# Two graph layers on one core: node tiles computed between the edge groups of the first layer

## Chip, cores and metric

One NeuronCore of a Trainium2 chip runs the whole program. The metric is the device time in microseconds (us) of one launch. Everything is float32.

## What is computed

There are 3125 nodes with 160 features (64 scalars, and 32 vectors of 3 components stored as `D = 64 + 96` columns) and 100,000 edges sorted by `dst`. Two message-passing layers follow each other, each with a residual and a layer norm. Cut to what matters here:

```python
# layer 0: gather f at src, sum over edges into dst
f_s, f_v = x_s @ Wl1_0 * a/8, einsum(x_v, Wl1_1) * a/sqrt(32)    # "f0", a = node_vec1
w0, w1, w2, w3 = split(gelu(gelu(ea8 @ Wfc1) @ Wfc2) @ Wfc3)
gs, gv = f_s[src], f_v[src];  y0, y1 = ea4[:, 0], ea4[:, 1:4]
mid0 = w0 * gs * y0
mid1 = w3 * einsum('euc,ec->eu', gv, y1) / sqrt(3)               # the dot product
mid2 = (w1 * gs)[:, :, None] * y1[:, None, :]
mid3 = w2[:, :, None] * gv * y0[:, None, None]
ns0, ns1, nv2, nv3 = segment_sum(..., dst) / sqrt(32)
x1 = layernorm(x + self_connection + alpha * out)                # per node; small matmuls of the sums
# layer 1: project x1, gather at dst, sum over edges into src
s, v, skip = x1 @ W_nl, x1 @ W_skip                              # per node
tp = tensor_product(relu(ea64 @ W_fc1) @ W_fc2, s[dst], v[dst], direction(ea3))
agg = segment_sum(tp, src);  out = layernorm(x1 + gate(agg @ W_out + skip))
```

## The kernel before

Edges are taken in groups of 512 (`G = 4` tiles of 128), 196 groups (`NGRP`). Nodes stand in 25 tiles of 128 rows (`NT`), in 5 chunks of 5 (`NC`, `FT`). Each engine has its own program; semaphores order them. The program has four stages.

**Prologue** (a block of its own, ended by a barrier of all engines). SP loads indices, then the small weights, then x; ACT's queue loads x transposed in two transfers. PE projects each node tile with both weight pairs side by side, so `ps_n` holds `f0` and the self connection; ACT scales the first half to `frow` (L293) and stores a chunk to `f0` in memory (L297); DVE adds the second half to `xres` (L382). Two PSUM buffers, so PE waits for both readers. POOL clears constants and the accumulators `acc_a`, `acc_b`, `acc_c`. DVE converts indices, counts whether every group's targets fit a window of 24 nodes (`win_ok`; with these inputs they do, so the `fast()` paths run), and works out edge directions in rows for a later table (`row_squares` to `row_dirs`).

**First layer**, 196 steps. POOL sends 4 indirect gathers for each group (L693), four groups ahead at most: group u waits for `prod_done` of group u - 4. PE runs three small MLP layers (`ps_h1`, `ps_h2` in a bank each, `ps_w`), ACT the two gelus. DVE builds a one-hot `ohot` and `sel` (one-hot times the 4 values of ea4), then three products of weights and gathered rows: `ta` (two copies of the scalars), `tb` (w3 times the 3 vector components) and `tc` (w2 times them). PE sums them into node windows (`window_sums`, L909): `ta` against all 4 copies of `sel`, `tb` against one, `tc` against three, 12 matmuls of two passes each. DVE adds the windows to the three accumulators (L1172). The dot product is thus taken after the sum over edges: ACT copies the diagonal blocks of `acc_c` onto each other later (L818). SP meanwhile clears the four output tables and writes the tables `hot_dst` and `hot_dir`.

**Node stage**, between joins 1 and 2 of all engines: for each node tile PE multiplies the sums (`update`), DVE adds to `xres`, takes mean and variance, ACT the square root, DVE a Newton step and the norm; PE transposes (`turn`) and projects (`project`); ACT copies out (`out_rows`), POOL spreads the row into `fst` (L716 to L724), SP stores it to `feat` and the skip part to table 0. Edge directions are worked out here too.

**Second layer**, 392 pairs of edge tiles (`NPAIR`): PE picks rows of `feat` with a one-hot (`window_gather`), forms the message; POOL adds messages into four tables in memory (L740, two indirect transfers a pair). An output stage adds the tables, gates and normalises.

The gather of the first layer, whose pace matters below:

```python
def gather(u, j, r):
    if r % 4 == 0:
        since(pool, gidx_done, j * 4 + r // 4 + 1)
    since(pool, prod_done, u - 3)
    for k in range(G):
        pool.indirect_dma_start(out=gat[:, r % 4, k, :], in_=t["f0"], ...).then_inc(gath[r % 4], 16)
```

## Time and profile before

| what | us |
|---|---|
| median of 3 runs (2736.01 to 2775.7) | 2751.35 |
| the profiled execution | 2767.32 |
| its span on the core | 2765.5 |

Times in the profile are microseconds from the start of the span. PE is TensorE's matmul, PEld its weight load, DVE VectorE, ACT ScalarE, POOL GpSimd, SP the engine that mostly issues transfers; SPq, ACTq are their transfer queues. PEclk is the granted TensorE clock as a share of full speed; 0.50 and 1.00 are its two levels. A row with xN merges N instructions from the start shown; "idle before <-" names what ended the idle time of the engine.

### The profile page before, as it was taken

The numbers are of one execution on the slowest core, as the hardware profiler recorded it, in microseconds if no ns is written. First come the engines' busy times: TensorE is split into PE (matmuls) and PEld (weight loads), VectorE is DVE, ScalarE is ACT, GpSimd is POOL, SyncE is SP. The second block draws the span as 40 slices with busy tenths as digits, with TensorE's granted clock in tenths as the row PEclk, the third lists the DMA queues.
The fourth block names the chain that finished last, engine by engine and source line by source line (L and its number), as shares of the span: only waits on it lengthen the run. The fifth ranks groups of instructions, "written<-read, shape, count | busy, mean of one in ns | idle before, by whom it ended". The sixth has DMA issues, their size and how long they took to land.

```text
span 2765.5 us, 80992 instructions
## 1 busy us (share of the span) xinstructions
PE 2655.6 (96%) x24330; PEld 2250.7 (81%) x24330; DVE 1649.6 (60%) x4264; ACT 899.5 (33%) x2015; POOL 2063.6 (75%) x1856
## 2 busy tenths in 40 slices
PE   4799999999999999999999999999999999999996
PEld 2477777777777777979999999999999999999993
DVE  5365555556555555526666666666666666666664
ACT  1111111111111112224444444444444444444442
POOL 3477777777777775247888888888888888888884
PEclk9999799889989898659999999999999999999998
DMA  4343343333433333247888888888888888888877
GB/s 132 111 110 105 100 109 106 100 104 105 108 103 105 105 105 85 104 173 142 141 144 144 141 144 143 144 143 143 143 142 143 143 144 142 144 144 142 144 124 189
DMA packets 388993, 355.59 MB, mean 129 GB/s; under 512 B 60992, under 2 KB 340928, under 8 KB 388416
## 3 DMA queue, kind: packets, MB, share of 16 engines
q0 software_dynamic: 150528, 141.40, 34.9%
q1 hardware_dynamic: 234816, 209.69, 27.2%
q10 hardware_dynamic: 3616, 4.11, 0.6%
q8 instruction: 15, 0.25, 0.0%
q14 instruction: 18, 0.15, 0.0%
HBM read 244.75 MB, written 135.90 MB: 138 GB/s over the span
## 4 chain that ended last, share of the span: by engine, by line
PE 65%; POOL 16%; issue 11%; DMA 3%; DVE 1%; DVEq 0%; ACT 0%; SPq 0%; POOLq 0%; ACTq 0%
POOL gat L693 15%; PE ps_o L1062 13%; PE ps_w L1050 12%; PE ps_d L1071 10%; PE ps_o L1060 9%; PE ps_x L1084 6%; PE ps_g L909 4%; PE ps_x L1024 3%; DMA gat<-f,gidx 2%; PE ps_w L935 2%; PE ps_h L928 1%; PE ps_h L923 1%; PE ps_r L981 1%; DMA tab<-summed,sidx 1%; PE ps_y L998 1%
## 5 line engine op out<-in xcount | busy, mean ns | idle before, releaser
L740 POOL DMA_INDIRECT tab<-summed,sidx x784 | 1218.6, 1554 | 264.5 <-issue 212.7
L693 POOL DMA_INDIRECT gat<-f,gidx x784 | 751.8, 959 | 244.8 <-issue 232.0
L1291 DVE TENSOR_TENSOR prod<-ps_w,xg 128x768 f32<-128x768 f32 x392 | 375.4, 958 | 244.5 <-PE ps_w L1050 226.7
L1062 PE MATMUL ps_o<-ro_v,prod 128*128 128x96 f32 x3136 | 478.5, 275 | 0.0
L1062 PEld LDWEIGHTS ps_o<-ro_v,prod 128*128 128x128 f32 x3136 | 413.3, 192 | 0.0
L1050 PE MATMUL ps_w<-hid,wf 64*128 64x128 f32 x4704 | 369.3, 290 | 2.0 <-ACT hid L864 2.0
L863 ACT ACTIVATE xg<-ps_x 128x768 f32<-128x768 f32 x392 | 296.3, 808 | 198.8 <-PE ps_x L1084 189.4
L1050 PEld LDWEIGHTS ps_w<-hid,wf 64*128 64x128 f32 x4704 | 294.1, 188 | 70.2 <-issue 44.6
L1071 PE MATMUL ps_d<-msg,same 128*128 128x193 f32 x1568 | 332.5, 334 | 0.7 <-ACT summed L882 0.7
L1060 PE MATMUL ps_o<-ro_s,prod 96*128 96x96 f32 x1568 | 330.2, 292 | 0.6 <-DVE msg L1302 0.6
L909 PEld LDWEIGHTS ps_g<-sel,ta 128*128 128x128 f32 x1568 | 210.0, 209 | 95.0 <-issue 59.2
L1160 DVE TENSOR_TENSOR ta<-ps_w,gat 128x512 f32<-128x512 f32 x196 | 135.5, 691 | 253.6 <-DMA gat<-f,gidx 191.2
L1060 PEld LDWEIGHTS ps_o<-ro_s,prod 96*128 96x128 f32 x1568 | 235.8, 190 | 48.1 <-issue 0.9
L876 ACT ACTIVATE msg<-ps_o 128x192 f32<-128x192 f32 x392 | 130.2, 332 | 443.6 <-PE ps_o L1062 424.5
L909 PE MATMUL ps_g<-sel,ta 128*128 128x96 f32 x1568 | 244.1, 304 | 21.3 <-DVE acc_c L1172 21.1
L785 ACT ACTIVATE h<-ps_h 128x256 f32<-128x256 f32 x196 | 75.1, 383 | 581.8 <-PE ps_h L928 576.8
L1071 PEld LDWEIGHTS ps_d<-msg,same 128*128 128x128 f32 x1568 | 247.9, 192 | 0.9 <-DVE msg L1302 0.9
L882 ACT ACTIVATE summed<-ps_d 128x386 f32<-128x386 f32 x392 | 193.1, 492 | 159.7 <-DMA tab<-summed,sidx 81.7
L1298 DVE TENSOR_TENSOR ash<-ps_o,sh 128x192 f32<-128x192 f32 x392 | 140.1, 357 | 137.6 <-ACT msg L876 131.1
L935 PE MATMUL ps_w<-w,h 64*128 64x192 f32 x1568 | 207.5, 388 | 0.0
L935 PEld LDWEIGHTS ps_w<-w,h 64*128 64x128 f32 x1568 | 143.2, 211 | 76.4 <-issue 76.4
L909 PE MATMUL ps_g<-sel,tc 128*96 128x72 f32 x1568 | 192.9, 272 | 0.0
(198 smaller groups left out, 3416.9 us busy)
## 6 DMA issues: line engine op xcount, KB each, us to landing
src_bc<-in_src_rows SPq DMA_DIRECT2D x196, 256.0 KB
tabw<-feat SPq DMA_DIRECT2D x784, 36.0 KB
ea<-in_ea SPq DMA_DIRECT2D x196, 128.0 KB
feat<-fst SPq DMA_DIRECT2D x25, 576.0 KB, 2.9
gat<-f,gidx POOLq DMA_INDIRECT x784
hot_dst<-in_dst_rows SPq DMA_DIRECT2D x98, 128.0 KB
hot_dir<-sh_rows SPq DMA_DIRECT2D x98, 128.0 KB
dst_bc<-hot_dst SPq DMA_DIRECT2D x196, 64.0 KB
```

What stands on the lines that cost most here:

```text
L693: pool.indirect_dma_start(out=gat[:, r % 4, k, :], out_offset=None, in_=t["f0"], in_offset=bass.IndirectOffsetOnAxis(ap=gidx[:, r // 4, at ...
L740: pool.indirect_dma_start(out=t["tabs"][into[k]], out_offset=bass.IndirectOffsetOnAxis(ap=sidx[:, r, k:k + 1], axis=0), in_=summed[:, r, k ...
L863: act.activation(xg[:, r, 2 * i:2 * i + 2, :], ps_x4[:, 2 * i:2 * i + 2, 0:3 * P], ACT.Copy)
L882: act.activation(summed[:, ur, :, :], ps_d[:, :, 0:LW], ACT.Copy).then_inc(sum_done, 1)
L909: last = pe.matmul(ps_g[r][0:hi, (n * 4 + lo) * WIN:(n * 4 + up) * WIN], lhs[:, r, k, :, :].rearrange("p a b -> p (a b)"), sel[:, r, k, lo ...
L935: last = pe.matmul(ps_w[r][:, k, 0:192], h2[h:h + S, r, P * (k % 2):P * (k % 2) + P], w3[h:h + S, :], start=True, stop=True)
L1050: last = pe.matmul(ps_w4[:, h, P * c:P * c + P], wf2[rows_h, c, :], hid[rows_h, r // 2, at], start=True, stop=True)
L1060: pe.matmul(ps_o[:, k, 0:96], prod[0:96, ur % 2, k, 0, :], ro_s[0:96, :], start=True, stop=True)
L1062: last = pe.matmul(ps_o[:, k, 96 + 64 * c:192 + 64 * c], prod[:, ur % 2, k, 1 + c, :], ro_v[:, c, :], start=True, stop=True)
L1071: last = pe.matmul(ps_d[:, k, 0:LW], same[:, ur // 2, ur % 2 * 2 + k, :], msg[:, ur % 2, k, :], start=True, stop=True)
L1084: last = pe.matmul(ps_x4[:, k, P * c:P * c + P], tabw[rows_k, r, CHUNK[c]:CHUNK[c] + P], hot[rows_k, r, :], start=True, stop=True)
L1291: dve.tensor_tensor(prod[:, r % 2, :, :, :].rearrange("p k c e -> p k (c e)"), ps_w4[:, :, 0:3 * P], xg[:, r // 2, r % 2 * 2:r % 2 * 2 + 2 ...
```

## The change

1. Prologue: weights are loaded first, x transposed comes in five pieces on ACT's queue. PE projects `f0` for all 25 tiles (`ps_n`, 4 buffers) before it projects the self connection for all 25 (`ps_m`, 3 buffers). ACT does its square roots after `f0`. POOL clears more (staging, weights, one accumulator of 5 x 3200) and then sends the first sixteen gathers (groups 0 to 3) inside the prologue, once `f0` is stored; `gather` skips them later. `win_ok` gains a check that the targets rise evenly enough.
2. First layer: DVE takes the dot product for each edge. `vy` = vectors times y1, `dot` its sum over components; `wy` = w2 times y0; `tb` now holds 3 blocks `wy * gv` and a fourth, w3 times `dot`. `window_sums` is 4 matmuls of `ta` against `sel` and 4 of `tb` against `ohot`; one accumulator `acc` and one addition a group. `ps_h1` and `ps_h2` share a bank, and `layer1(u)` waits for the second gelu of the group before.
3. Node tiles are worked on in the edge loop, now unrolled by 8 (`PER`): tile t gets its sums copied out at DVE's step 8(t+1)+5 (`node_parts`), PE's `update`, `turn`, `project` at steps 0, 4, 6 of block t+2, DVE's `node_update`, `node_scale`, `node_norm`, `node_turned`, `node_staged` at 0, 1, 2, 4, 6, and ACT's spreading into `fst` and store to `feat` at steps 2 to 4 of block t+3 (POOL has no part in it). The inverse root is made on DVE alone, from a shift and three Newton steps. 23 tiles go through the loop, the last two into the first pairs of the second layer. Loads of later weights go into the loop's first steps. One join is left of two.
4. The skip part goes to table 0 in ten transfers on SP's queue in the second layer's first steps; the scatters start with tables 2 and 3, and pair 1 waits for all ten.

The diff, cut to its core:

```diff
 @block.gpsimd  (prologue)
+                pool.memset(fst[:, :, :, :], 0.0).then_inc(fst_zero, 1)
+                pool.memset(acc[:, :, :], 0.0).then_inc(zeroed, 1)
...
+                pool.wait_ge(gidx_done, 1)
+                pool.wait_ge(f_out[0], 16 * (-(-NC // 2)))
+                pool.wait_ge(f_out[1], 16 * (NC // 2))
+                for u in range(4):
+                    for k in range(G):
+                        pool.indirect_dma_start(
+                            out=gat[:, u, k, :], out_offset=None, in_=t["f0"],
...
 @block.tensor  (prologue)
                 for u in range(NT):
...
+                    since(pe, f_ready, u - 3)
+                    pe.matmul(ps_n[u % 4][:, 0:S], xt_s[:, here], w_s2[:, 0, :], start=True, stop=True)
+                    pe.matmul(ps_n[u % 4][:, S:D], xt_v[:, here], w_v2[:, 0, :], start=True, stop=True).then_inc(n_ready, 1)
+                for u in range(NT):
+                    since(pe, res_ready, u - 2)
+                    pe.matmul(ps_m[u % 3][:, 0:S], xt_s[:, here], w_s2[:, 1, :], start=True, stop=True)
+                    pe.matmul(ps_m[u % 3][:, S:D], xt_v[:, here], w_v2[:, 1, :], start=True, stop=True).then_inc(m_ready, 1)
 def window_sums(pe, r, ready):
-                for n, (lhs, hi, lo, up) in enumerate(((ta, P, 0, 4), (tb, 96, 0, 1), (tc, 96, 1, 4))):
-                    for k in range(G):
-                        last = pe.matmul(ps_g[r][0:hi, (n * 4 + lo) * WIN:(n * 4 + up) * WIN],
...
+                for k in range(G):
+                    pe.matmul(ps_g[r][:, 0:4 * WIN], ta[:, r, k, :, :].rearrange("p a b -> p (a b)"),
+                              sel[:, r, k, :, :].rearrange("p a b -> p (a b)"), start=k == 0, stop=k == G - 1)
+                for k in range(G):
+                    last = pe.matmul(ps_g[r][:, 4 * WIN:5 * WIN], tb[:, r, k, :, :].rearrange("p a b -> p (a b)"),
+                                     ohot[:, r, k, :], start=k == 0, stop=k == G - 1)
 def layer1(u, r, j):
-                    since(pe, g1_done, u)
+                    since(pe, g2_done, u)
 def products(u, j, r):   (DVE)
+                    dve.tensor_tensor(vy[:, :, :, :], gv, y[:, bass.ds(u * G, G), 1:4]..., ALU.mult).then_inc(vy_done, 1)
                     dve.wait_ge(w_ready, u + 1)
                     dve.tensor_tensor(ta[:, h, :, :, :], ...)
+                    dve.tensor_tensor(wy[:, :, :], ps_w[h][:, :, 2 * S:2 * S + V], ...).then_inc(wy_done, 1)
+                    dve.wait_ge(vy_done, u + 1)
+                    dve.tensor_reduce(dot[:, :, :], vy[...].rearrange("p k c u -> p k u c"), AX.X, ALU.add).then_inc(dot_done, 1)
+                    dve.wait_ge(wy_done, u + 1)
+                    dve.tensor_tensor(tb[:, h, :, 0:3, :], wy[:, :, :].unsqueeze(2)..., gv, ALU.mult)
+                    dve.wait_ge(dot_done, u + 1)
+                    dve.tensor_tensor(tb[:, h, :, 3, :], ps_w[h][:, :, 2 * S + V:2 * S + 2 * V], dot[:, :, :],
+                                      ALU.mult).then_inc(prod_done, 1)
 def fast(), step(s, j, r):   (DVE)
+                        if r == 5 and (not isinstance(j, int) or 0 <= j - 1 < TIN):
+                            since(dve, acc_done, s - 1)
+                            node_parts(j - 1)
+                        tile = j - 2
+                        if not isinstance(tile, int) or 0 <= tile < TIN:
+                            if r == 0:
+                                node_update(tile, 0)
+                            if r == 1:
+                                node_scale(tile, 1)
+                            if r == 2:
+                                node_norm(tile, 1)
+                            if r == 4:
+                                node_turned(tile, 0)
+                            if r == 6:
+                                node_staged(tile, 0)
+                def node_parts(u):
+                    dve.tensor_copy(tile_sums[:, :, :], acc[:, :, here]).then_inc(part_done, 1)
+                def node_scale(u, n):
+                    linked(last)
+                    linked(dve.tensor_scalar(var, mv[:, 0:n, 1], EPS, None, ALU.add))
+                    linked(dve.tensor_scalar(tmp.bitcast(I32), var.bitcast(I32), 1, None, ALU.logical_shift_right))
+                    linked(dve.tensor_scalar(y.bitcast(I32), tmp.bitcast(I32), -1.0, float(0x5f3759df), ALU.mult, ALU.add))
+                    for _ in range(2):
+                        linked(dve.tensor_tensor(tmp, y, y, ALU.mult))
+                        linked(dve.tensor_tensor(tmp, tmp, var, ALU.mult))
+                        linked(dve.tensor_scalar(tmp, tmp, -0.5, 1.5, ALU.mult, ALU.add))
+                        linked(dve.tensor_tensor(y, y, tmp, ALU.mult))
 second layer
+                            if nodes_left:
+                                for u in range(LAST, NT):
+                                    turn(u, u - LAST)
+                        if nodes_left and isinstance(s, int) and s == 2:
+                            project(NT - 1, 1, NT)
+                            pe.wait_ge(y_done, NT)
...
+                    if isinstance(g, int) and g == 0:
+                        for m in range(NC - 1):
+                            store_skip(m)
+                    if isinstance(g, int) and g == 1:
+                        sp.wait_ge(y_done, NT)
+                        store_skip(NC - 1)
...
-                    into = [(r * 2 + k) % NTAB for k in range(2)]
+                    into = [(r * 2 + k + 2) % NTAB for k in range(2)]
+                    if isinstance(u, int) and u == 1:
+                        pool.wait_ge(skip_out, 16 * 2 * NC)
```

`linked` makes DVE wait for each instruction's own end before the next (12 links in `node_scale`, 4 in `node_norm`). `window_hot(0)` and `window_hot(1)`, and the loads of the second layer's first window, are made ahead of the join.

## Rows read from the trace of the kernel before

**Rows 1.** The page: costliest groups, busy us, mean ns | idle before, releaser.

```profile
...
L740 POOL DMA_INDIRECT tab<-summed,sidx x784 | 1218.6, 1554 | 264.5 <-issue 212.7
L693 POOL DMA_INDIRECT gat<-f,gidx x784 | 751.8, 959 | 244.8 <-issue 232.0
```

**Rows 2.** Waits of the whole span: us in total, times, longest.

```profile
...
POOL gat L693 <- DVE tc L1164: 12.7, 23, 3.4
```

**Rows 3.** Timeline at full, then half clock: start, us, engine, instruction.

```profile
...
1050.05 1.13 PE L909 MATMUL ps_g<-sel,ta 128*128 128x96 f32 x8 [0.92 <-DVE acc_c L1172]
...
1054.41 1.13 PE L909 MATMUL ps_g<-sel,ta 128*128 128x96 f32 x8
...
1070.85 2.02 PE L909 MATMUL ps_g<-sel,ta 128*128 128x96 f32 x8
...
1079.00 2.02 PE L909 MATMUL ps_g<-sel,ta 128*128 128x96 f32 x8
```

**Rows 4.** 5 us windows: busy of PE, PEld, DVE, ACT, POOL; PEclk, DMA.

```profile
...
495.00:500.00 5.00, 4.32 (x37) 3.36 (x37) 2.73 (x8) 0.87 (x3) 3.78 (x5) 1.00 0.48 139
500.00:505.00 5.00, 5.00 (x21) 3.26 (x20) 2.73 (x8) 0.77 (x2) 3.78 (x5) 0.51 0.27 66
```

**Rows 5.** Window in the first layer, columns as in rows 4.

```profile
...
200.00:400.00 200.00, 196.59 (x1454) 156.89 (x1454) 110.19 (x315) 31.80 (x90) 151.86 (x159) 0.89 0.40 105
```

**Rows 6.** Timeline, end of the first layer and node stage.

```profile
...
1098.36 0.22 DVE L1172 TENSOR_TENSOR acc_c<-acc_c,ps_g 96x72 f32 x1
...
1102.30 0.41 PEld L977 LDWEIGHTS ps_r<-r_s,acc_a 128*128 128x128 f32 x2
...
1102.90 0.16 DVE L1223 TENSOR_TENSOR alpha<-ps_r,a_col 128x1 f32<-128x1 f32 x1
...
1104.03 0.16 DVE L1223 TENSOR_TENSOR alpha<-ps_r,a_col 128x1 f32<-128x1 f32 x1
1104.08 0.41 PEld L977 LDWEIGHTS ps_r<-r_s,acc_a 128*128 128x128 f32 x2
...
1111.62 0.17 DVE L1443 TENSOR_TENSOR ntmp<-rstd 128x5 f32<-128x5 f32 x1
...
1111.82 0.17 DVE L1444 TENSOR_TENSOR ntmp<-ntmp 128x5 f32<-128x5 f32 x1
```

**Rows 7.** Timeline, start of the second layer.

```profile
...
1231.70 0.34 DVE L1334 COPY msg<-rank_i 128x1 f32<-128x1 f32 x4 [22.22 <-SPq L633]
...
1235.22 1.66 PE L1084 MATMUL ps_x<-hot,tabw 32*128 32x128 f32 x24 [4.23 <-DMA tabw<-feat]
```

**Rows 8.** Timeline of the prologue.

```profile
...
15.22 8.09 POOL L253 MEMSET acc_c<- 96x9600 f32 x1
15.58 8.15 DVE L313 CAST src_f<-src_i 128x784 f32<-128x784 int32 x1 [15.46 <-DMA base_i<-in_dst_first]
...
25.52 0.96 DVE L323 TENSOR_REDUCE ext<-rel_f 128x1 f32<-128x784 f32 x1
...
67.35 0.56 DVE L348 TENSOR_TENSOR f<-f 112x384 f32<-112x384 f32 x1 [6.50 <-DMA f<-in_ea_rows]
```

**Rows 9.** Window of the prologue's node loop, columns as in rows 4.

```profile
...
33.40:83.30 49.90, 38.80 (x94) 23.60 (x94) 28.14 (x48) 11.26 (x26) 0.00 (x0) 1.00 0.19 60
```

**Rows 10.** Timeline, 75 to 112 us: first layer's start.

```profile
...
87.53 0.19 POOL L677 MEMSET w<- 16x128 f32 x1 [64.23 <-POOLq L172]
...
100.25 1.21 PE L923 MATMUL ps_h<-ea,w 16*128 16x256 f32 x2 [17.62 <-DMA ea<-in_ea]
...
110.02 0.94 POOL L693 DMA_INDIRECT gat<-f,gidx  x1 [0.88 <-DVE tc L1164]
```

**Rows 11.** Groups by form, 200 to 1000 us: busy us, mean ns, idle before.

```profile
...
L1164 DVE TENSOR_TENSOR tb<-ps_w,gat 128x384 f32<-128x384 f32 x158 | 86.4, 547 | 0.0
...
L1172 DVE TENSOR_TENSOR acc_b<-acc_b,ps_g 96x24 f32 x158 | 26.4, 167 | 0.0
```

**Rows 12.** Transfers: issuing line, size, us to landing.

```profile
...
tab<-skrow SPq DMA_DIRECT2D x5, 480.0 KB, 4.0
```

More of the change, by code:

```diff
@@ L1020, in hidden @@
-                def hidden(g, r, turn):
-                    pe.wait_ge(ea_in[r], 16 * (turn + 1))
+                    pe.wait_ge(r_ok, 6)
+                    pe.wait_ge(wn_in2, 16 * 8)
+                    pe.wait_ge(acc_done, NGRP * SWEEP)
+                    for u in range(NT):
+                        since(pe, y_done, u)
+                        update_last(u, 0)
+                        turn(u, 0)
+                        project(u, 0)
+                def hidden(g, r, times):
+                    pe.wait_ge(ea_in[r], 16 * (times + 1))
@@ new lines, in general, with window_hot @@
+                    pad_rows()
+                    steps(dve, NGRP, step, 8, 4)
+                    inverse()
+                    directions()
+                    for u in range(NT):
+                        node_update(u, 0)
+                        node_scale(u, 1)
+                        node_norm(u, 1)
+                        node_turned(u, 0)
+                        node_rows(u, f1[:, u, :], f1_done)
+                    first_hot()
+                def window_hot(g, r, turn):
+                    dve.wait_ge(hot_in[r], 32 * (turn + 1))
+                    since(dve, x_ready, g - 1)
+                    dve.scalar_tensor_tensor(hot[:, r, :], dst_bc[:, r, :], slot_f[:, bass.ds(g, 1)], dir_bc[:, r, :],
+                                             ALU.is_equal, ALU.mult).then_inc(hot4_done, 1)
@@ L1335, in second_layer @@
                     dve.wait_ge(rank_set, 4)
-                    window_hot(0, 0, 0)
-                    window_hot(1, 1, 0)
+                    if not sweep:
+                        for u in range(LAST, NT):
+                            node_update(u, u - LAST, NT)
                     if sweep:
```

894 lines of the change are left out of this document (477 added, 417 removed).

## The prediction, made before the changed kernel ran

> **What bounds the kernel now.** I read the page first, for how its costliest lines are paced; then the waits of POOL, the groups of the first layer by form, the windows by stage, and last the timelines at each change of stage.
>
> The page shows two lines of POOL that fill two stages. 784 gathers are busy for 751.8 us, and 232.0 us more go to issue between them: 1.255 us a gather, 5.02 us a group of four, 984 us for the stage [rows 1]. The reader is to see that nothing else ends POOL's idle time: DVE made it wait 12.7 us in all [rows 2]. The second layer is alike: 784 scatters take 1218.6 + 264.5 us; without the 20 us before the first, that is 1.87 us each, two a pair, 1463 us. So POOL paces both layers, and an engine beside it matters only when it falls behind by more than the buffers.
>
> PE is close behind. At full clock the sums of one group start 4.36 us after those of the last (1050.05, 1054.41); at half clock 8.15 us (1070.85, 1079.00) [rows 3]. The clock is 1.00 while PE is busy 4.32 of 5 us, and falls to its half level in the next window [rows 4]; over 200 us its mean is 0.89, so some 22% of the time is at half [rows 5]. PE then falls behind POOL, and the four gather buffers carry it until it has caught up. DVE is busy 110.19 of 200 us, 2.77 us a group [rows 5].
>
> Between the layers lie 133 us in which POOL moves no edge: the last addition ends at 1098.6, the second layer's first DVE instruction starts at 1231.7 [rows 6, 7].
>
> **Prologue.** DVE's first conversion takes 8.15 us and ends 0.4 us after POOL's clearing that began beside it [rows 8]. A conversion of 784 columns can't need that: it waited for the clearing. POOL now clears 16,000 accumulator columns instead of 25,600; at acc_c's rate (9600 in 8.09 us) that is 13.5 us, after about 4.5 us of smaller clearings, so DVE is let go near 20 instead of 23.7, and its longer checks (two reductions of 196 columns at 0.96 us per 784, and four small ones) give 1.6 us back: 31.4 instead of 33.4. The node loop then takes 49.9 us, of which DVE works 28.1 [rows 9] and waits once 6.5 us for edge rows [rows 8]; the rest are waits for ACT and PE that alternate with it on two buffers. With `f0` done before (25 tiles at about 0.8 us, PE's and ACT's time together, from near 10 us) these waits go: 31.4 + 28.1 + 6.5 = 66, and 4.3 us more to the barrier as now (83.2 to 87.53). I take 71 against 87.5: **-16** (bounds -5, if late pieces of x or the square roots behind `f0` hold DVE, and -25).
>
> **Early gathers.** Sixteen gathers are 16 x 1.255 = 20 us of POOL. But the seventeenth waits for the products of group 0: it starts at 110.02 after a wait of 0.88 us for DVE, 22.5 us after the barrier, and PE's first matmul of the stage waits until 100.25 for a transfer behind SP's weight loads [rows 10]. This chain is not moved. POOL will be done early and wait 20 us. **-1** (bounds +1 and -20).
>
> **Edge loop.** POOL: unchanged, 5.02 us a group. PE: the four `tc` sums go, the `tb` sums load 128 columns instead of 96; of 2.4 us for 24 passes 16 are left, some 0.4 us less at full clock. A node tile adds one `update` (1.78 us with an idle matmul in it [rows 6]), two transposes, one `project` and three pauses, about 4 us, 0.5 a group: 4.4 at full and about 8.1 at half clock, as before. The shared bank of `ps_h` costs nothing while the second gelu (0.4 us) runs under `layer3` (0.9); uncovered it is 0.4 a group, still under 5.02.
> DVE: two products of 384 columns stay two (`vy` and `tb` for `tb` and `tc`, 547 ns [rows 11]). `wy` and the fourth block of `tb` add 0.2 us each (128 columns, near the 167 ns row [rows 11]), the reduction of 384 columns 0.47 by the row of 784 [rows 8]; three additions become one, -0.24. 2.77 + 0.63 = 3.4. A node tile: `node_update` 1.13 (1102.90 to 1104.03), 16 linked operations at 0.20 (1111.62 to 1111.82) 3.2 [rows 6], the copy of 640 columns 0.7, norm and copy back 0.6, turning and staging 1.2: 6.8 us in 27 instructions, 0.85 a group. Together **4.25 of 5.02**. Both are hidden, but in bursts: with `node_scale` a step of DVE takes 6 us, which eats PE's lead and slows the recovery after a fall of the clock. No row shows this. The least is that the present 12.7 us of stalls go (-13); I take stalls of 28 us, **+15**; the upper bound is the clock rival below. If the cover is gone, 0.1 us a group costs 20 us. ACT gains nine short copies a tile, 2.5 of 40 us, with none of POOL's node work left; SP's extra loads stand in the first steps, where `ea8` is one step ahead.
>
> The row of the conversion shows more: a copy of DVE in SBUF and work of POOL exclude each other [rows 8]. In the loop nine of the 27 node instructions are such copies or scalar operations, beside gathers, which hold POOL 0.96 of 1.255 us [rows 1]. The trace has no such pair. The Trainium skill (SBUF — State Buffer, "Who interferes with whom") says that DVE in its two-port modes and GpSimd block each other for the whole instruction, whoever came first, and that copy, cast and tensor_scalar can enter these modes. By this rule the conversion waits for the clearing, as the row has it; for the loop it speaks against the change, and the sum would be that of the third or the fourth rival instead of mine. I take no wait, since no row prices one behind a gather; both ends are kept.
>
> **Node stage and join.** 133.1 us go. In their place after the last sums stand: `project` of tile 22 (1.3), two `update`s (3), the three idle matmul groups of the join (2.6) and `hidden` (0.6), while ACT spreads tile 22 beside it (nine copies, 2.5). PE's first `window_gather`, now at 1235.22 after 4.2 us for `tabw` [rows 7], which is loaded ahead now, would come at 1105.6: **-130** (bounds -120 and -133).
>
> **Second layer's start.** DVE's `node_scale` and `node_norm` of two tiles (4.6 us) stand before pair 1, turning and two projections before the sums of pair 1: about 7 us until the first scatter. On SP's queue eight skip transfers stand before the window of group 2; a table chunk took 4.0 us to land [rows 12] and the half rows are no cheaper, so 16 us of queue: 5 us more for PE's third gather. Since POOL paces what follows, none of it is caught up: **+12** (bounds +3 and +25). The rest of the layer and the output are unchanged.
>
> **Sum.** -16 - 1 + 15 - 130 + 12 = -120 on the profiled 2767.3: 2647. That execution lies 16 us above the median, so **2631** against 2751.35.
>
> **Rivals.**
> *The clock falls more often.* PE's idle before a fall is small [rows 4], and DVE's bursts make more of it. With 40% of the time at half clock PE needs 1 / (0.6/4.4 + 0.4/8.1) = 5.38 us a group: 196 x 0.36 = 71 us of stalls instead of 28: **2674**. Against it: PE's work is the same as before.
> *Early gathers pay, stalls go.* If the start chain is shorter without gathers on the DMA rings and DVE's slack suffices: -28 and -19, **2584**. For it: `y` and `ea8` land behind gathers now. Against: SP's order.
> *Node instructions wait for half a gather each.* 0.5 x 0.96 x 0.77 = 0.37 us, 27 times, is 1.25 a group: DVE needs 5.5, 100 us of stalls for 28: **2703**.
> *Slower.* One mechanism: each node instruction of DVE waits for a whole gather, 0.96 us, since a linked chain lets the next gather in between. 27 x 0.96 / 8 = 3.2: DVE needs 7.5 us a group, and the loop costs 484 us for 28: **3087**. It decides from a loss of 120 us on: 5.78 us a group, or 0.45 us of wait per instruction. For it: the conversion's row; against: its partner was one long clearing, and gathers leave 0.3 us between them.
>
> **Chances.** Forecast 0.57, clock 0.16, early gathers 0.10, half a gather 0.10, slower 0.07. The forecast's own range by its bounds is 2600 to 2665. The range 2580 to 2700 takes in the clock and the early gathers and leaves out the two port cases, 0.17, less what of the half case falls inside. Two per cent (what this kernel's runs can tell from no change) is 55 us, 2696: faster 0.86, same 0.08, slower 0.06.
>
> **What would show it.** POOL's waits for DVE in the loop near 28 us and gathers 1.255 us apart (else the clock or the port); the seventeenth gather about 22 us after a barrier near 71; DVE near 4.25 us a group, its linked operations 0.20 apart (0.5 or more: the port); mean clock near 0.88 (0.8: the clock rival); 7 to 10 us from the last sums to the join; the first scatter 25 to 30 us behind it, then 3.73 us a pair. The prediction is wrong if DVE or PE, and not POOL, sets the pace of the loop, or if an unpriced start of the second layer takes more than 25 us.

## The result: 15% slower, and the profile after

Measured: **3179.21 us** median for the changed kernel beside 2753.38 for the one before, ratio 1.154 with a 95% interval of 1.145 to 1.162. The forecast was 2631, faster. Another execution of the same kernel (`after_again`, 3200.34 us beside 2746.41, ratio 1.166, 1.154 to 1.179; profiled span 3209.2) is the one read here, since the first profile lies 47 us above the others of its kernel.

From its page: POOL's two costliest lines and the row of the granted clock (tenths of full speed, 40 slices of 80 us).

```profile
PE   7799999999999999999989999999999999999996
POOL 4355554445554444444328888888888888888884
PEclk5555655555665555555579999999999999999998
L776 POOL DMA_INDIRECT tab<-summed,sidx x784 | 1229.0, 1568 | 302.8 <-issue 213.7
L756 POOL DMA_INDIRECT gat<-f,gidx x768 | 754.5, 982 | 741.3 <-DVE tb L1249 541.9
```

The gathers are as short as before (982 ns, 959 in [rows 1]), but POOL stands 741.3 us between them, 541.9 of it waiting for DVE's last product of an older group; in the kernel before it waited 12.7 us for DVE in all [rows 2]. POOL no longer paces the first layer. DVE does not either. The windows by stage (PE, weight loads, DVE, ACT, POOL busy with counts; clock; DMA share; GB/s):

```profile
400.00:600.00 200.00, 195.05 (x792) 150.77 (x788) 113.30 (x331) 24.29 (x87) 105.30 (x108) 0.54 0.29 79
600.00:800.00 200.00, 200.00 (x769) 154.32 (x770) 110.12 (x314) 24.03 (x87) 98.33 (x101) 0.50 0.27 75
```

DVE is busy 110 of 200 us, PE all 200, and the clock is at 0.50, the 1.2 GHz level. PE's own rows from the first profile of the changed kernel show its period (start, us, line, shape, count):

```profile
507.64 2.02 PE L964 MATMUL ps_g<-sel,ta 128*128 128x96 f32 x8
509.46 1.79 PE L967 MATMUL ps_g<-ohot,tb 128*128 128x24 f32 x8
511.08 1.20 PE L984 MATMUL ps_h<-h,w 128*128 128x256 f32 x2
512.21 1.66 PE L991 MATMUL ps_w<-w,h 64*128 64x192 f32 x8
513.80 1.22 PE L979 MATMUL ps_h<-ea,w 16*128 16x256 f32 x2
514.94 2.02 PE L964 MATMUL ps_g<-sel,ta 128*128 128x96 f32 x8
```

From 507.64 to 514.94 is 7.3 us a group with no gap, and with the node steps' matmuls 101 gathers are sent in 200 us, 7.9 us a group. At full clock before it was 4.36 [rows 3].

The same profile has one interval at full clock (1020 to 1055 us), and there the kernel is what was forecast: the 256 columns of L979 take 426 ns instead of 709, and from 1025 to 1055 POOL sends 24 gathers in 30 us, 5.0 us a group.

```profile
1025.00:1055.00 30.00, 28.03 (x203) 21.88 (x202) 25.35 (x76) 6.38 (x24) 22.96 (x24) 1.00 0.41 108
```

What ends such an interval can be read too. after_again has two of them, near 378 to 415 us and 866 to 904 us. At the end of the first, PE stands 4.95 us at the `turn` of a node tile, waiting for `x1b`, the last product of DVE's node chain, and the clock falls:

```profile
410.00:415.00 5.00, 2.06 (x17) 1.43 (x16) 3.61 (x10) 0.84 (x5) 3.78 (x5) 1.00 0.60 193
415.00:420.00 5.00, 3.00 (x10) 2.02 (x11) 4.03 (x14) 0.38 (x1) 3.78 (x5) 0.56 0.41 121
417.00 0.39 PE L1018 MATMUL ps_p<-ident,x1b 128*64 128x128 f32 x1 [4.95 <-DVE x1b L1345]
```

The other interval of this profile and the one of the first profile end with the same wait, of 4.90 and 5.03 us. In the kernel before, the longest wait of PE ahead of each of its falls from 200 us on is 0.7 to 1.6 us, for `acc_c`.

Where the time went, in the profiles (us; the points are POOL's seventeenth gather, DVE's last addition to the accumulators, POOL's first scatter, the end). bf_before and bf_after are the kernel before and the changed one with 16-bit operands, from the experiments below.

| part | before | after_again | difference | predicted | bf_before | bf_after | difference |
|---|---|---|---|---|---|---|---|
| to the 17th gather | 110.0 | 110.5 | +0.4 | -16 - 1 | 109.6 | 110.4 | +0.8 |
| to the last addition | 988.6 | 1507.6 | **+519.0** | +15 | 980.5 | 1009.0 | +28.6 |
| to the first scatter | 153.2 | 39.7 | **-113.4** | -130 + 12 | 117.1 | 36.5 | -80.6 |
| to the end | 1513.7 | 1551.4 | +37.7 | 0 | 1519.9 | 1541.8 | +21.9 |
| span | 2765.5 | 3209.2 | +443.7 | -120 | 2727.1 | 2697.7 | -29.4 |

### The profile page after: what moved, and what is told of

Its sections match the earlier page's. It is cut to its first block, busy times and chain, and to the rows that moved or that the text cites. A ratio compares the mean times of both kernels' runs of the same rounds, so it can differ in the third digit from the quotient of the medians.

```text
span 3224.9 us, 78018 instructions
## 1 busy us (share of the span) xinstructions
PE 3134.4 (97%) x22818; PEld 2589.0 (80%) x22818; DVE 1889.4 (59%) x4945; ACT 893.0 (28%) x2126; POOL 2031.5 (63%) x1632
## 4 chain that ended last, share of the span: by engine, by line
PE 64%; POOL 12%; issue 10%; DMA 8%; SPq 1%; DVE 1%; POOLq 1%; ACT 0%; DVEq 0%; ACTq 0%
POOL tab L776 12%; PE ps_g L964 12%; PE ps_g L967 9%; PE ps_w L991 9%; DMA tab<-summed,sidx 7%; PE ps_h L979 7%; PE ps_h L984 6%; PE ps_o L1141 4%; PE ps_w L1123 4%; PE ps_d L1152 3%; PE ps_o L1139 3%; PE ps_x L1165 2%; PE ps_x L1098 1%; PE ps_p L1012 1%; SPq L723 1%
## 5 line engine op out<-in xcount | busy, mean ns | idle before, releaser
L1141 PE MATMUL ps_o<-ro_v,gat 128*128 128x96 f32 x3136 | 480.0, 276 | 0.0
L1464 DVE TENSOR_TENSOR gat<-ps_w,xg 128x768 f32<-128x768 f32 x392 | 375.4, 958 | 140.3 <-PE ps_w L1123 111.3
L1141 PEld LDWEIGHTS ps_o<-ro_v,gat 128*128 128x128 f32 x3136 | 415.0, 192 | 0.0
L964 PE MATMUL ps_g<-sel,ta 128*128 128x96 f32 x1568 | 388.1, 427 | 0.0
L967 PEld LDWEIGHTS ps_g<-ohot,tb 128*128 128x128 f32 x1568 | 350.3, 327 | 0.0
L967 PE MATMUL ps_g<-ohot,tb 128*128 128x24 f32 x1568 | 344.5, 371 | 0.0
L1139 PE MATMUL ps_o<-ro_s,gat 96*128 96x96 f32 x1568 | 331.0, 293 | 13.8 <-DVE msg L1475 11.5
L1152 PE MATMUL ps_d<-msg,gat 128*128 128x193 f32 x1568 | 333.8, 335 | 4.1 <-ACT summed L936 3.8
L1139 PEld LDWEIGHTS ps_o<-ro_s,gat 96*128 96x128 f32 x1568 | 236.6, 190 | 63.8 <-issue 20.7
L1152 PEld LDWEIGHTS ps_d<-msg,gat 128*128 128x128 f32 x1568 | 248.2, 192 | 5.9 <-issue 5.2
```

Of the source, the lines that this page charges most:

```text
L964: pe.matmul(ps_g[r][:, 0:4 * WIN], ta[:, r, k, :, :].rearrange("p a b -> p (a b)"), sel[:, r, k, :, :].rearrange("p a b -> p (a b)"), star ...
L967: last = pe.matmul(ps_g[r][:, 4 * WIN:5 * WIN], tb[:, r, k, :, :].rearrange("p a b -> p (a b)"), ohot[:, r, k, :], start=k == 0, stop=k == ...
L1139: pe.matmul(ps_o[:, k, 0:96], prod[0:96, ur % 2, k, 0, :], ro_s[0:96, :], start=True, stop=True)
L1141: last = pe.matmul(ps_o[:, k, 96 + 64 * c:192 + 64 * c], prod[:, ur % 2, k, 1 + c, :], ro_v[:, c, :], start=True, stop=True)
L1152: last = pe.matmul(ps_d[:, k, 0:LW], same[:, ur // 2, ur % 2 * 2 + k, :], msg[:, ur % 2, k, :], start=True, stop=True)
L1464: dve.tensor_tensor(prod[:, r % 2, :, :, :].rearrange("p k c e -> p k (c e)"), ps_w4[:, :, 0:3 * P], xg[:, r // 2, r % 2 * 2:r % 2 * 2 + 2 ...
```

## How far the clock record can be trusted

The clock row must be read with a duration beside it. In the kernel before, the stretch from 98 to 120 us is shown at clock 1.00, and yet its matmuls of 256 columns take what they take at half clock (by form: count, busy, mean ns, idle):

```profile
98.00:120.00 22.00, 18.33 (x64) 11.71 (x64) 5.59 (x12) 3.17 (x9) 16.07 (x17) 1.00 0.45 125
L923 PE MATMUL ps_h<-ea,w 16*128 16x256 f32 x8 | 4.9, 709 | 17.6 <-DMA ea<-in_ea 17.6
L928 PE MATMUL ps_h<-h,w 128*128 128x256 f32 x8 | 4.8, 704 | 1.4 <-ACT h L781 1.4
```

So the kernel before also began its first layer at half clock and rose near 125 us. In what follows, half clock means 704 to 709 ns for these two lines, full clock 420 to 426. The Trainium skill (TensorE: Matmul & The Clock Gate, "Seeing it yourself") warns that the records of the clock are not fully reliable on this chip; the rows above agree.

## Experiments

Kernels sent together ran on one chip beside the kernel before. On two of the chips used here the kernel before took about 2750 us, on three about 3200; each was used once, so it is not shown that the chip makes the difference and not the hour. Each result therefore stands beside before's time on its own chip.

### The sums alone, and the node steps alone (before: 2746)

`before_notc`: the kernel before without its third sums, and without their addition to `acc_c` on DVE (not printed here).

```diff
-for n, (lhs, hi, lo, up) in enumerate(((ta, P, 0, 4), (tb, 96, 0, 1), (tc, 96, 1, 4))):
+for n, (lhs, hi, lo, up) in enumerate(((ta, P, 0, 4), (tb, 96, 0, 1))):
```

> Kernel before with its third sums over edges (tc, 4 matmuls of 72 columns per group) and their addition to acc_c left out, so the third part of the messages is missing from the result; DVE's product tc stays. No node work in the loop, the prologue as before. Theory 1 (with these sums goes what brought the clock back): the clock stays at 0.50 for most of the first layer, PE's period is 6.9 to 7.3 us instead of 8.15, and the kernel takes 2950 to 3150 us, slower than before although it does less. Theory 2 (node steps in the loop hold the clock down) and theory 3 (the state that the new prologue leaves): the clock comes back as in before, POOL's 5.02 us sets the pace, 2650 to 2750 us.

`nonode`: the changed kernel with all node tiles but the first behind the loop.

```diff
-TIN = (NGRP - 20) // PER + 1
+TIN = 1            # TSTAGE too; the steps in the loop run for tile 0 only
```

> Changed kernel with the node tiles but the first taken out of the loop over groups; they run in the loop that the changed kernel has behind it for the last tiles, one after the other. Nothing is left out. Theory 1: the clock stays at 0.50 in the first layer, period 7.3 us, and the serial node tiles add some 7 us each: about 3180 - 195*0.5 + 19*7 = 3220 us, at least 3100. Theory 2 (node steps hold the clock down): the clock is at 1.00 for most of the first layer, period 5.0 to 5.4 us, so 195*2.4 = 470 us less and the serial node tiles back: 2750 to 2850 us.

> The changed kernel once more, for a profile of an execution near its median. Both theories say 3175 to 3190 us, granted clock 0.50 in nearly the whole first layer, PE busy in all of it, PE's period 7.3 us per group of edges outside the steps with node work and about 7.8 over eight groups. If the clock is at 1.00 in more than a fifth of the first layer while the time is still near 3180, the clock is not the cause.

Measured: before_notc **3101.55** (ratio 1.130, 1.121 to 1.139), nonode **3399.51** (1.239), after_again 3200.34 (1.166). before_notc, then nonode, 400 to 600 us:

```profile
400.00:600.00 200.00, 200.00 (x820) 149.46 (x816) 77.83 (x203) 23.01 (x66) 116.91 (x117) 1.00 0.30 77
400.00:600.00 200.00, 200.00 (x770) 153.05 (x770) 98.16 (x246) 21.31 (x60) 110.56 (x110) 0.50 0.28 71
```

```profile
L923 PE MATMUL ps_h<-ea,w 16*128 16x256 f32 x6 | 3.6, 709 | 0.0
L928 PE MATMUL ps_h<-h,w 128*128 128x256 f32 x6 | 3.6, 704 | 0.0
```

The clock row of before_notc says 1.00; its durations (the second fence, 500 to 520 us) say half, and 117 gathers in 200 us are 6.84 us a group. The kernel before, with nothing changed but these sums and their addition, does less and becomes 355 us slower, because PE no longer leaves the half level. This happens with the old prologue and without node steps in the loop, so neither the new prologue nor the node steps are needed for it. nonode never rises either, at 110 gathers, 7.27 us a group: the node steps don't keep the clock from rising, though they end the intervals in which it has risen. They are worth 199 us where they are, even at half clock.

PE's time at half clock adds up: 6.84 for the old work without `tc`; the `tb` sums with 128 columns of weights take 8 x (377 - 323 ns) = 0.43 more (means of one matmul in nonode and before_notc), which is nonode's 7.27; the node steps add 0.65 and give the 7.9 of after_again. The prediction said 8.1.

### A hot start (before: 3223)

```diff
+idle_matmuls(pe, ps_h[:, :], ident[:, :], 16)   # ahead of the first layer
 pe.wait_ge(w_in, 16 * 6)
```

> Changed kernel with 16 matmuls of 512 columns of identity ahead of the first layer, while PE waits for its weights there. Theory 3 (the state at the start decides, and a clock that is once at full speed stays): the first layer runs at full clock, the period is 5.0 to 5.4 us, 2600 to 2750 us. Theory 1 (the loop's own work decides): the clock is at full for the first groups, falls within some 100 us and doesn't return; 3150 to 3190 us.

Measured: **3290.51** (1.022, 1.010 to 1.034). Its windows from 98 us on:

```profile
98.00:103.00 5.00, 5.00 (x13) 2.20 (x12) 1.28 (x3) 0.00 (x0) 0.00 (x0) 1.00 0.41 151
103.00:108.00 5.00, 2.67 (x8) 0.86 (x6) 0.00 (x0) 2.13 (x4) 0.00 (x0) 1.00 0.06 11
108.00:113.00 5.00, 4.46 (x14) 2.44 (x14) 0.93 (x3) 0.79 (x3) 0.00 (x0) 0.61 0.47 143
```

The layer begins at full clock, PE waits for half of a window in the first groups, the clock falls, and it stays at half in all but three of the 298 windows of 5 us from 110 to 1600 us (their mean is 0.502). A high clock at the start alone is not enough. This is also the nearest there is to the changed kernel on a chip where before takes 3200 us: 2% slower than before there, not 15%.

### Work given to PE (before: 2746 for fill384; 3199 and 3223 for the others)

`fill384` puts one matmul of 384 columns into each group, which nothing reads; fill768 has two, fill1152 three, and `before_fill` two of 192 columns in the kernel before.

```diff
 since(pe, acc_done, u - 1)
+pe.matmul(ps_g[ur % 2][:, 128:512], ident[:, :],
+          ident[:, :].unsqueeze(1).to_broadcast([P, 3, P]), start=True, stop=True)
 window_sums(pe, ur % 2, agg_done)
```

> Changed kernel with one matmul of 384 columns more per group, of identity into unused columns of the sums' bank, ahead of the window sums (nothing reads it). Theory 1, the sums that were dropped kept the array busy enough for the clock to come back: the first layer shows the granted clock at 1.00 most of the time, PE adds 0.64 us per group at full clock (3.6 + 0.64 = 4.2 us, under POOL's 5.02), the period falls from 7.8 to 5.0 to 5.4 us, and the kernel takes 2600 to 2700 us. Rival, something else than the clock's return holds PE (gelus, a wait on DVE or the node steps), and PE merely has more work: PE adds 1.28 us per group at half clock, 195 groups, so 3180 + 250 = 3430 us with the clock still at 0.50.

> Changed kernel with two matmuls of 384 unused columns per group. One brought 3061 us: at full clock PE then idles beside POOL and the clock falls again. Theory 1: with two PE has 3.6 + 1.3 = 4.9 us of work per group at full clock, nearly POOL's 5.02, so it hardly idles, the clock stays at 1.00 for over four fifths of the first layer, and the kernel takes 2600 to 2720 us. Rival (the filler brings the clock back only by chance of its place): no better than one, 3000 to 3250 us.

> Changed kernel with three matmuls of 384 unused columns per group. Theory 1: PE has 3.6 + 1.9 = 5.5 us per group at full clock and never waits there, so the clock stays at 1.00; PE sets the pace at 5.5 to 5.7 us, 0.5 to 0.7 above POOL's, 195 groups: 2700 to 2800 us. It costs more than fill768 if that one already holds the clock, and less if not.

> Kernel before with 384 unused columns per group (two matmuls of 192) ahead of its window sums. Theory 1: PE has 4.36 + 0.64 = 5.0 us per group at full clock, about POOL's 5.02, so the intervals at half clock, 22% of its first layer, go or shrink: 5.38 to about 5.1 us per group, 195 groups, 2690 to 2720 us, faster than before although it does more. Rival (half-clock intervals come by themselves, whatever PE does): they stay, each group at half clock costs 1.3 us more: 2800 us.

> fill768 once more, for the same reason (3263 us beside 3199 for before, granted clock 0.81 in the loop, PE standing for some 4 us at each of 43 falls). On a chip where before takes 2750 us and falls ten times in 700 us: fewer falls, 5.2 to 5.8 us per group, 2640 to 2800 us. If it is at the mercy of the filler alone: 3250 us again.

| kernel | us | before there | mean clock in the loop | falls | over |
|---|---|---|---|---|---|
| before | 2751 | | 0.875 | 10 | 695 us |
| after_again | 3200 | 2746 | 0.522 | 2 | 1200 us |
| fill384 | 3061 | 2746 | 0.716 | 14 | 1200 us |
| before_again | 3212 | 3215 | 0.676 | 37 | 1300 us |
| fill768 | 3263 | 3199 | 0.811 | 43 | 1300 us |
| fill1152 | 3226 | 3199 | 0.890 | 37 | 1300 us |
| before_fill | 3221 | 3199 | 0.766 | 35 | 1200 us |

(A fall is counted where the clock of one 5 us window is over 0.75 and that of the next is not.) fill384 does more than the changed kernel and is 139 us faster beside the same runs of before: with it the clock comes back again and again.

```profile
800.00:1000.00 200.00, 192.41 (x1108) 143.43 (x1107) 143.29 (x425) 32.51 (x118) 130.89 (x135) 0.86 0.38 101
```

135 gathers in 200 us are 5.93 us a group. This is its best stretch; over the whole loop it is 7.03, beside 7.68 for after_again. It falls 14 times, and its two runs lie at 3033 and 3089 (the one profiled): an aid, no cure, and no gain over the kernel before. The expectation of 2600 to 2700 missed, as theory 1 said nothing of what ends a full-clock interval. The trace does. Sixteen times PE comes to a tile's `turn` at full clock in the loop. Fifteen times it waits 1.8 to 2.7 us for `x1b` there, and the clock falls within 2 us of that wait; the one time that it doesn't wait, at 1485 us, full clock goes on for 12 us. One of the fifteen:

```profile
404.48 0.39 PE L1018 MATMUL ps_p<-ident,x1b 128*64 128x128 f32 x1 [2.23 <-DVE x1b L1347]
```

A `turn` placed later in the block, when `x1b` is ready, is the obvious next experiment; it was not run.

On the other chips neither two nor three fillers got under before: fill768_b, on a third chip, took 3289.75 (1.022), near the 3250 of its rival; a chip where before takes 2750 us, which it was meant for, it did not get. before_fill did not gain either (1.007, 0.998 to 1.016): its mean clock is 0.766, beside 0.676 for before on a like chip, but PE has more work, and it falls 35 times; what takes the gain away was not worked out.

### The same work put back (before: 3199, 3223 and 3215)

`tc_back` is the changed kernel with four matmuls of 72 columns in place of those that went. `notc_fill` is before_notc with four matmuls of the old shape on identity, `notc_tb` the same on real numbers. The edit of notc_tb:

```diff
+for k in range(G):
+    pe.matmul(ps_g[ur][0:96, 320:392], tb[:, ur, k, :, :].rearrange("p a b -> p (a b)"),
+              sel[:, ur, k, 1:4, :].rearrange("p a b -> p (a b)"), start=k == 0, stop=k == G - 1)
 window_sums(...)
```

> Changed kernel with just the array work back that the change took off PE: 4 matmuls of 72 columns per group with tb as the weights, into unused columns of the sums' bank, which nothing reads. Theory 1 (the clock comes back only with that work): durations at half clock as in the kernel before, the period at half clock 7.3 + 1.1 = 8.4 us outside the node steps, and intervals at full clock as in the kernel before, where POOL's 5.02 us sets the pace; with the quarter at half clock that before had, 5.02*0.75 + 8.6*0.25 = 5.9 us or less per group, so 2650 to 2850 us, faster than the changed kernel although PE does more. Rival (the change's other parts hold the clock down): the clock stays at 0.50 and the kernel takes 3180 + 195*1.1 = 3400 us.

> tc_back once more, since on another chip the kernel before took 3199 us where it had taken 2746. There it stayed at half clock: 9.4 us per group instead of 7.8, 3566 us. If the chip decides, on a chip where before takes 2750 us the clock comes back and it takes 2650 to 2900 us; if the rest of the change does (a node step, the wider weights of tb), it stays at half clock and takes 3450 to 3570 us on any chip.

> Kernel before without its third sums (as in before_notc, so a third part of the messages is missing), with 4 matmuls of 96 columns of weights and 72 columns in their place, of identity, into unused columns of the bank. Theory 1 (it is the work of the array that brings the clock back, whatever it computes): the half-clock intervals look as in the kernel before, and so does the time, within 2% of it. Rival (the data, the waits or the addition on DVE that went with the sums matter): as before_notc, 13% over before, with the 256-column matmuls at 704 to 709 ns throughout.

> As notc_fill (third sums' result left out), but with real numbers in the four matmuls: tb as weights and sel as columns, the shapes and order of the sums that were taken out. If the numbers that stream matter, or the margin on which the clock came back in before is in them: as the kernel before within 3%, where notc_fill was 5% over it with the clock at half throughout. Rival (what went with the addition on DVE decides): as notc_fill, over 4% above before.

Measured: tc_back **3565.68** (1.116) and **3545.35** on another chip (1.101), notc_fill **3371.56** (1.047, 1.035 to 1.059), notc_tb **3370.53** (1.049, 1.042 to 1.056). None comes back to full clock for long. Both notc kernels stay at half, 8.1 us a group; tc_back rises twice and tc_back_b six times, each time for 13.7 us, in the first 1900 us. notc_tb gives PE the shapes of the kernel before, but not quite its order: the four matmuls stand ahead of the `ta` sums and not behind the `tb` sums. An addition on DVE is missing too, and the numbers are others. Before rose 36 times on the same chip and notc_tb did not. So my theory that the array's work by its shapes decides is not enough, and three expectations of mine fell with it; the order, the addition and the numbers are not told apart. What is shown is weaker: the kernel before flips between the levels by itself, and several small edits, of less work or of the same, leave it at the low one. Which property of PE's work brings the clock back is **open**.

### Why before takes 3200 us on some chips

> Kernel before once more, for a profile on a chip where it takes 3200 us instead of 2750. If the clock makes that difference: the same durations at either clock (256 columns in 426 or 709 ns), half-clock intervals in 50 to 70% of the loop instead of 22%, 7.5 to 7.8 us per group, POOL waiting for DVE more. Rival (another engine or the memory is slower on that chip): the pace at full clock is above 5.0 us.

Measured: **3212.11** (0.997, 0.992 to 1.002). Its loop at 400 to 600 us, and one of the 5 us windows in which PE shows almost no work:

```profile
400.00:600.00 200.00, 174.86 (x976) 136.56 (x976) 75.98 (x221) 20.70 (x61) 104.95 (x108) 0.70 0.27 71
365.00:370.00 5.00, 0.27 (x1) 0.16 (x1) 0.92 (x3) 0.03 (x1) 2.51 (x3) 0.62 0.26 66
```

The half-clock share is 65%, as expected, but that is not all: at 14 of the 37 falls PE's records have a hole of 3.0 to 4.5 us, where before on the other chips shows none above 1.6 us at its falls. fill1152 shows what is in one:

```profile
493.09 0.68 PE L984 MATMUL ps_h<-h,w 128*128 128x256 f32 x2
499.35 0.38 ACT L820 ACTIVATE h<-ps_h 128x256 f32<-128x256 f32 x1 [8.38 <-remote]
499.88 0.76 PE L979 MATMUL ps_h<-ea,w 16*128 16x256 f32 x1 [5.25 <-ACT h L820]
```

The matmul is recorded as done at 493.77, and ACT, which waits for just that, starts at 499.35. PE's ends are modelled in a profile; whatever the array did, its result was handed on over 5 us late. On the chips where before takes 2750 us no wait of this kind ("remote") is found from 200 to 1000 us in any of the profiles.

### PE taken out of the way

`nosums` and `before_nosums` (before: 3215) sum one of four tiles only (`for k in range(1)` in `window_sums`).

> Changed kernel with the sums over edges made from the first of a group's four tiles alone: 2 of the 8 matmuls per group, so three quarters of the messages are missing from the result. It tells what the rest of the change is worth where PE can't be the bound. At half clock PE has 7.3 - 3.8 + 1.0 = 4.5 us per group and 0.8 of node work, so about POOL's 5.02. If the prediction's other steps hold (POOL's 5.02 us per group, DVE beside it, node stage gone): 2620 to 2700 us, whatever the clock. Rival (something besides PE's clock holds the changed kernel, the dot product's chain on DVE or the node links): over 2800 us, with POOL waiting for DVE.

> Kernel before with the same cut: 3 of its 12 matmuls for the sums per group, three quarters of the messages missing. PE at half clock has 8.15 - 5.0 + 1.4 = 4.5 us per group, under POOL's 5.02, so its loop costs 5.0 to 5.1 us per group instead of 5.38: 2751 - 195*0.35 = 2680 us. The prediction gave the change -135 us beside the loop's pace and +15 within it; it would then be about 50 to 120 us above nosums.

Measured: **3121.21** (0.972, 0.963 to 0.981) and **3080.92** (0.959, 0.951 to 0.968). The changed one is 40 us behind the other, where 50 to 120 us ahead was expected, but on that chip this settles little: both kernels send a group every 7.3 and 6.7 us, far over POOL's 5.02, with PE's records busy only three quarters of the time.

`bf_after` and `bf_before` (before: 2754.29) keep all the work and halve PE's passes for the sums and the third layer instead:

```diff
-            ta = sb(c2, "ta", [P, 2, G, 2, S])
+            ta = sb(c2, "ta", [P, 2, G, 2, S], BF)   # bfloat16; so sel, tb, ohot (before: tc), h2, w3
```

> Changed kernel with the operands of its sums over edges and of the third layer of the edge network (ta, tb, sel, ohot, h2, w3) in 16-bit floats instead of 32; nothing is left out, but the numbers are rounded. PE needs one pass instead of two for 16 of its 20 matmuls per group: at half clock about 2.4 us for the first two layers, 0.6 for the third, 1.3 for the sums, 0.8 of node work, so 5.1 us instead of 7.8. Theory (TensorE at half clock is what holds the changed kernel, and the rest of the prediction stands): POOL's 5.02 us per group sets the pace even at half clock, 2620 to 2720 us where the kernel before takes 2750; on the chips where PE stands for some 5 us again and again and before takes 3200, 2650 to 3000. Rival (a DVE chain or the node links hold it): over 3050 us on any chip, with POOL waiting for DVE as in after.

> Kernel before with the same operands (ta, tb, tc, sel, h2, w3) in 16-bit floats. PE at half clock has some 4.5 us per group, so POOL's 5.02 sets the pace of its loop at either clock: 2680 us where the kernel before takes 2750. If the prediction's steps beside the loop hold (node stage -130, start of the second layer +12, loop 0 against this kernel), it is 50 to 130 us above bf_after; if bf_after isn't under it by 50 us, the prediction was wrong on the node work too.

Measured: bf_after **2698.29** (0.980, 0.974 to 0.987), bf_before **2734.47** (0.994, 0.989 to 0.998). bf_after at 400 to 600 us, POOL's points in it, and the first scatter of bf_before:

```profile
400.00:600.00 200.00, 157.75 (x729) 87.14 (x728) 164.22 (x482) 36.09 (x129) 152.85 (x155) 0.50 0.42 118
```

```profile
110.37 1.31 POOL L757 DMA_INDIRECT gat<-f,gidx  x1 [20.93 <-DVE tb L1250]
1109.97 0.95 POOL L757 DMA_INDIRECT gat<-f,gidx  x1 [0.30 <-issue]
1155.89 1.63 POOL L777 DMA_INDIRECT tab<-summed,sidx  x1 [30.05 <-DVE sidx L1486]
```

```profile
1207.21 1.67 POOL L741 DMA_INDIRECT tab<-summed,sidx  x1 [20.29 <-DVE sidx L1313]
```

This settles the main question. The clock is at 0.50 throughout the loop, as in nearly all of the changed kernel's, but PE needs less than POOL, and 500 us are gone: POOL is busy 152.85 of 200 us, a group costs (1109.97 - 110.37) / 191.75 = 5.21 us with its node steps (767 gathers from the seventeenth on), and the kernel takes 2698. That DVE got faster by the smaller type is no rival: its products take what they took in 32 bits (`ta` 684 and 692 ns for 691, `tb` 548 for 547). bf_before is at half clock in its whole loop as well, by its durations (709 and 704 ns for the two 256-column lines, over all 392 of each; its clock row says 1.00), and its loop takes 980.5 us, no more than before's 988.6.

PE stands at each of the 23 `turn`s of bf_after's loop for 5.0 to 6.4 us, and since POOL paces the kernel, this does not show in its pace.

The rest of the forecast holds only in part. 2698 lies inside its range of 2580 to 2700, but by 2 us, and the gain over its pair is 36 us between the medians and 29 in the profiles, a quarter of the 120 forecast. The expectation of bf_before had set the mark at 50 us, under which the prediction was wrong beside the clock too: it was. (The 16-bit versions round the sums, to a relative error of 0.06, so they are no replacement for either kernel.)

## Why the prediction was wrong, point by point

**The step that failed** is in the edge loop: "4.4 at full and about 8.1 at half clock, as before", with the share of time at half clock taken over from before, 22%. The pace at half clock was right (7.9). At full clock POOL set the pace in the one full interval, at 5.0 us a group, with PE busy 28.03 of 30 us, 4.7 a group where 4.4 was forecast. The share was wrong: 96% (mean 0.522 over 240 windows of 5 us from 400 to 1600 us in after_again). 0.96 x 7.9 + 0.04 x 5.0 = 7.8 us a group is 2.76 over POOL's 5.02, 530 us of stalls for 192 groups where the prediction had 28. Less the 13 us of the kernel before that is 517; the table has +519, where the term of the sum was +15. The rival "the clock falls more often" had the right place, but it let the share grow from 22 to 40% by more falls. It was right on what makes a fall: DVE's burst of node work, for which PE waits at `turn`, a wait that the prediction did not price. But there are only two such falls in 1200 us. What cost the time is that the clock did not rise. The sentence against it, "PE's work is the same as before", took equal time for equal work: PE needs 8.1 us a group at half clock in both kernels, but with other matmuls in it. before_notc shows that taking the `tc` sums and their addition out is enough by itself: it is 355 us over before, after_again 454 on the same chip. Why the clock then stays low is open.

The error of method: an alternating clock was treated as a fixed tax. A kernel whose PE is 96% busy and yet goes up and down ten times in 695 us shows a state that can tip, and its half-clock pace of 8.15 us stood in [rows 3], 3 us above POOL's. 195 groups at 8.1 instead of 5.0 are 600 us; that was the price of a rival that I left out, and the rows at hand were enough for it.

**Prologue, -16: measured 0.** The barrier is at 87.72 (87.53 before; these figures are from the first profile). DVE was let go at 19.98 as forecast, but `f0` takes 0.61 + 0.67 = 1.28 us a tile on PE where I took 0.8, and the second pass as much again, until 86.5. Half clock alone does not explain that, since the kernel before was there too (607 ns for its matmuls of 192 columns, 564 at half clock in before_notc's loop). It is the split: side by side both pairs took 38.80 us for 23 tiles [rows 9], 1.7 a tile; in two passes of narrower matmuls they take 2.6. The edge rows of the second half land at 70.49 after DVE has waited 8.79 us for them, and their arithmetic stands between the last skip sums.

**Early gathers, -1: right.** The seventeenth starts at 110.45, after 22.17 us of waiting for DVE, beside 110.02.

**DVE in the loop: its work right, its stalls not.** bf_after, at POOL's pace, has DVE busy 164.22 of 200 us, 4.24 a group where 4.25 was forecast. Its loop costs +28.6 beside bf_before, where +15 was forecast, but not by the stalls that +15 stood for: behind the seventeenth gather POOL waits 5.8 us for DVE in bf_after, 14.6 in bf_before. 22 us of the 28.6 are longer gathers, 993 ns for 964 in the mean.

**The port rivals: refuted.** The linked operations of the node chain stand 0.19 to 0.20 us apart in the trace of the changed kernel, as in [rows 6]:

```profile
408.49 0.15 DVE L1323 TENSOR_SCALAR ntmp<-ntmp 128x1 int32<-128x1 int32 x1
408.68 0.15 DVE L1324 TENSOR_SCALAR rstd<-ntmp 128x1 int32<-128x1 int32 x1
```

The rule of the Trainium skill that I weighed (SBUF — State Buffer, "Who interferes with whom") says that copies of DVE in the two-port modes and GpSimd block each other for the whole instruction. Against the long clearing it agrees (the conversion again ends with it); beside gathers no wait of that size shows. What shows is on POOL's side, and small: the gathers take 982 ns for 959 (993 for 964 in the 16-bit pair). The longer ones don't lie beside the node instructions: of the 117 over 1000 ns in after_again's loop 112 overlap DVE's new product `vy` (L1237), which overlaps 191 in all. Whether `vy` is the cause was not tried.

**Node stage and start of the second layer, -130 + 12 = -118: measured -113.4** from the last addition to the first scatter. Between the two 16-bit kernels it is -80.6, since bf_before does its node stage in 117.1 us where before takes 153.2: from 1100 to 1200 us bf_before's mean clock is 0.90, before's 0.62. So 36 us of what the node stage costs before is the clock too.

**The rest of the second layer, 0: measured +37.7** (bf pair +21.9). Scatters take 1568 ns for 1554, 11 us for 784. The remainder is in waits whose cause was not tried: from 1800 to 2200 us ACT waits 166.6 us for additions to the tables in bf_after, 0.4 in bf_before.

## What to carry to other kernels

When TensorE's clock alternates, work out the loop's pace at the low level and compare it with the engine that paces the kernel. If it is above it, the kernel's time hangs on a state that an edit can tip either way, and the price of "half clock throughout" belongs among the rivals, whatever the edit saves. What worked here was not filler but to bring PE's time at the low level under the pacing engine's, at the price of rounding; then the level hardly matters (bf_before's loop at half clock takes 980.5 us, before's, mostly at full, 988.6). And where PE must wait for another engine inside the loop, look at what its clock does behind that wait. Before believing a clock row, look at the duration of one matmul shape that occurs at both levels.

## What the runs showed of the hardware that I had not expected

- TensorE can stay at its 1.2 GHz level for 1200 us while its records show it busy in all of them (nonode, 200 to 1400 us: none of 240 windows over 0.50). The Trainium skill (TensorE: Matmul & The Clock Gate, "What's actually happening") has the throttled state as the default that activity releases; here being busy in the records was not enough.
- Taking matmuls out of a loop made the kernel slower by 13% (before_notc), and putting useless ones in made one faster by 4% (fill384, 3061 for 3200).
- In fill384 the clock falls with every wait of PE of 1.8 to 2.7 us at a `turn` reached at full clock, 15 of 15 in the loop; in the changed kernel it falls with all three such waits, of 4.9 to 5.0 us.
- The same kernel takes 2750 us on some chips and 3200 on others. On one of the latter its clock falls 37 times in 1300 us, with a hole of 3.0 to 4.5 us in PE's records at 14 of the falls, where the profile of a 2750 us chip has ten falls in 695 us and no such hole.
